# Rounding h0 on ScalarE instead of VectorE, and taking all of group 1's batch sums to VectorE, in a fused condition and feed-forward kernel

## What is computed

```python
# x: 32 batches x 64 rows x 512; cond: 32 x 256; W_fc: 2048 x 512; W_proj: 512 x 2048
q_emb = relu(cond @ W3 + b3)                       # one row of 512 per batch
x1    = (n * x + x.sum(axis=rows)) * q_emb         # n = 64 rows per batch
h0    = relu(x1 @ W2 + b2)
h     = square(relu(h0 @ ternary(W_fc).T))         # 2048 wide
hn    = h * rsqrt(mean(square(h)) + eps)
out   = x + hn @ ternary(W_proj).T
# ternary(w): groups of 64 weights; scale = mean |w|, q = clip(round(w / scale), -1, 1), result q * scale
```

## Time and profile before

| | |
|---|---|
| device time, median of 3 runs | 312.59 us (312.39 to 313.21) |
| device time of the profiled execution | 312.75 us |
| its span | 311.0 us |
| what lies around the span | 1.75 us (312.75 - 311.0) |
| TensorE (PE) busy | 305.5 us, 98% of the span |
| VectorE (DVE) busy | 188.7 us, 61% |
| ScalarE (ACT) busy | 191.1 us, 61% |
| GpSimd (POOL) busy | 102.0 us, 33% |

### The profile page before, as it was taken

How to read it: one execution, slowest core, us unless ns; L and a number is a source line. 1 busy time by engine, 2 the same in 40 slices (tenths; PEclk the granted TensorE clock), 3 DMA queues, 4 the chain that set the end, 5 groups by cost and what they waited for, 6 DMA issues and landing times.

```text
span 311.0 us, 3798 instructions
## 1 busy us (share of the span) xinstructions
PE 305.5 (98%) x1286; PEld 233.7 (75%) x1286; DVE 188.7 (61%) x318; ACT 191.1 (61%) x282; POOL 102.0 (33%) x94
## 2 busy tenths in 40 slices
PE   8999999999999999999999999999999999999995
PEld 7764545446888888888888888888888888888883
DVE  0589999995778877888348235952223484222245
ACT  1685366696999699977646554445555445555540
POOL 1012333345433223344342431253333314333330
PEclk9999999999999999999999999999999999999999
DMA  6999435443464041115004300340000033000003
GB/s 211 354 274 277 173 73 99 133 112 93 125 212 103 1 102 37 34 34 52 17 0 147 125 0 1 133 140 0 0 2 0 0 135 137 0 0 0 2 2 136
DMA packets 31332, 27.03 MB, mean 87 GB/s; under 512 B 18736, under 2 KB 20816, under 8 KB 31312
## 3 DMA queue, kind: packets, MB, share of 16 engines
q1 hardware_dynamic: 29936, 26.22, 29.8%
q10 hardware_dynamic: 1376, 0.56, 0.7%
HBM read 18.39 MB, written 4.19 MB: 73 GB/s over the span
## 4 chain that ended last, share of the span: by engine, by line
PE 98%; DVE 0%; issue 0%; POOL 0%; POOLq 0%; DVEq 0%
PE ps_out L360 37%; PE ps_acc L348 37%; PE ps_acc L332 18%; PE ps_out L310 2%; PE ps_out L319 1%; PE ps_acc L404 1%; PE ps_x L419 1%; PE ps_acc L411 0%; PE ps_x L394 0%; DVE x_sb L565 0%; DVE x_t L495 0%; PE ps_x L400 0%; PE ps_acc L407 0%; POOL ident_f L712 0%; POOL ident_f L710 0%
## 5 line engine op out<-in xcount | busy, mean ns | idle before, releaser
L243 POOL TENSOR_TENSOR wv_sb<-wv_sb 128x512 f32<-128x512 f32 x55 | 71.7, 1304 | 122.7 <-DVE y_lo L510 115.6
L348 PE MATMUL ps_acc<-h_hi,w_t 128*128 128x512 f32 x256 | 100.0, 391 | 0.0
L360 PE MATMUL ps_out<-w_t,y_hi 128*128 128x512 f32 x256 | 100.0, 391 | 0.0
L360 PE MATMUL ps_out<-w_t,y_lo 128*128 128x512 f32 x256 | 99.6, 389 | 0.0
L348 PE MATMUL ps_acc<-h_lo,w_t 128*128 128x512 f32 x256 | 99.6, 389 | 0.0
L508 DVE CAST y_hi<-x_t 128x512 fp32r<-128x512 f32 x64 | 33.2, 518 | 86.9 <-PE ps_out L360 70.2
L655 ACT ACTIVATE x_t<-ps_acc 128x512 f32<-128x512 f32 x64 | 37.8, 591 | 61.1 <-PE ps_acc L348 61.1
L332 PE MATMUL ps_acc<-x_t,wv_sb 128*128 128x512 f32 x128 | 56.3, 593 | 0.3 <-DVE x_t L495 0.3
L348 PEld LDWEIGHTS ps_acc<-h_lo,w_t 128*128 128x128 f32 x256 | 48.1, 188 | 10.2 <-issue 0.2
L348 PEld LDWEIGHTS ps_acc<-h_hi,w_t 128*128 128x128 f32 x256 | 48.1, 188 | 10.2 <-issue 0.2
L360 PEld LDWEIGHTS ps_out<-w_t,y_hi 128*128 128x128 f32 x256 | 48.1, 188 | 9.9
(11 more groups left out here) (61 smaller groups left out, 163.6 us busy)
## 6 DMA issues: line engine op xcount, KB each, us to landing
x_sb<-in_x_dram SPq DMA_DIRECT2D x5, 1024.0 KB, 5.3
raw<-in_L_ffn_W_fc_dram SPq DMA_DIRECT2D x8, 512.0 KB, 7.0
raw<-in_L_ffn_W_proj_dram SPq DMA_DIRECT2D x8, 512.0 KB, 4.2
out_dram<-x_sb SPq DMA_DIRECT2D x16, 256.0 KB, 2.1
x_odd<-in_x_dram SPq DMA_DIRECT2D x2, 1024.0 KB, 7.6
x_sb<-in_x_dram SPq DMA_DIRECT2D x4, 256.0 KB, 4.2
wv_sb<-in_L_cond_W_dram SPq DMA_DIRECT2D x4, 256.0 KB, 8.7
x_t<-in_L_cond_W_dram ACTq DMA_DIRECT2D x1, 512.0 KB, 4.6
```

The lines of the kernel that those rows point to most:

```text
L243: engine.tensor_tensor(acc, acc, y_sq[:, v % SQ_RING, :], ALU.add).then_inc(sq_added, 1)
L348: last = pe.matmul(ps_acc[:, (UNITS + v) % ACC_RING, :], w_t[:, j, k * P:(k + 1) * P], part[:, k, g * BANK:(g + 1) * BANK], start=(k == 0 ...
L360: last = pe.matmul(ps_out[:, t, :], part[:, v % RING, t * P:(t + 1) * P], w, start=(opens(v) and part is y_hi), stop=(closes(v) and part i ...
```

## The change

It has four parts. All of group 1 is transposed, with sums by VectorE (`sums_by_vector`). `round_h0` is gone: `relu_h0` on ScalarE reads the PSUM bank twice, once for `h0_hi` and once for `h0_f`, and VectorE keeps only a wait where its cast stood. Step 1 moves from unit 1 to unit 2, where it stands behind group 1's blocks. GpSimd's subtraction of unit u also waits until VectorE has done its work of unit u (`vector_through`).

```diff
-    STEP_AT_UNIT = {0: 0, 1: 1, 3: 2, 7: 3, 9: 4, 11: 5, 12: 6, 14: 7}
+    STEP_AT_UNIT = {0: 0, 2: 1, 3: 2, 7: 3, 9: 4, 11: 5, 12: 6, 14: 7}
...
     def sums_by_vector(g, k):
-        return g > 1 or g == 1 and k > 1
+        return g > 0
...
+    def blocks_scaled(u):
+
+        return KD + len([k for v in range(min(u + 1, UNITS - KD)) for k in SUMS_OF_UNIT[v // KD][v % KD]])
...
+        def vector_through(u):
+
+            steps = [v for v in STEP_AT_UNIT if v <= u]
+            last_scale = max([v for v in range(min(u + 1, UNITS - KD)) if SUMS_OF_UNIT[v // KD][v % KD]], default=-1)
+            if max(steps) >= last_scale:
+                return tern_ready, len(steps)
+            return x1_ready, blocks_scaled(u)
...
-            def round_h0(u):
-                g, m = u // KD, u % KD
-                dve.wait_ge(h0_relued, u + 1)
-                dve.tensor_copy(h0_hi[:, m, g * BANK:(g + 1) * BANK], h0_f[:, u % RING, :]).then_inc(h0_hi_done, 1)
-
...
                 if u > 0:
-                    round_h0(u - 1)
+
+                    dve.wait_ge(h0_relued, u)
...
-            round_h0(UNITS - 1)
...
             def relu_h0(u):
-                m = u % KD
+                g, m = u // KD, u % KD
                 act.wait_ge(h0_done, u + 1)
+                act.activation(h0_hi[:, m, g * BANK:(g + 1) * BANK], ps_acc[:, u % ACC_RING, :], ACT.Relu, bias=bv_t[:, m:m + 1]
+                               ).then_inc(h0_hi_done, 1)
                 wait(act, h0_split, u - RING + 1)
                 act.activation(h0_f[:, u % RING, :], ps_acc[:, u % ACC_RING, :], ACT.Relu, bias=bv_t[:, m:m + 1]
                                ).then_inc(h0_relued, 1)
...
                 pool.wait_ge(h0_hi_done, u + 1)
+                pool.wait_ge(h0_relued, u + 1)
+                pool.wait_ge(*vector_through(u))
```

## The result

| | before | after |
|---|---|---|
| median of the runs compared | 312.49 us (311.87 to 313.21, 4 runs) | 315.45 us (315.28 to 315.95, 4 runs) |
| profiled execution, its span | 312.75, 311.0 us | 315.28, 313.3 us |

The ratio is 1.0100, with a 95% interval from 1.0082 to 1.0118. The changed kernel is slower by 2.96 us; +2.23 was forecast, a time of 314.8 in a range of 313.4 to 316.3.

What follows compares the result with a forecast made beforehand. TensorE's own list of work, busy 98% of the span, was taken as the bound. Terms -0.91 + 1.36 + 0.69 + 0.70 + 0.39 = +2.23 us on 312.59 gave 314.8, range 313.4 to 316.3.

Steps and rivals of the forecast that it cites:

- The order on VectorE as the cause: On VectorE, pair 2's reduce and scales come behind group 1's four blocks, so ScalarE's w_scale and queued h0 hold TensorE.
- the first two stalls: TensorE waits for ScalarE's h0: 1.36 us at make_h0(5) and 0.69 at make_h0(6).
- handovers of 3.70 us: VectorE's reduce and scales, then ScalarE's w_scale and h0 writes: 1.49 + 0.96 + 0.58 + 0.67 us per turn.
- the small waits in the tiles (0.39): Two or three short TensorE stalls ahead of project(2), (4) and (6), together 2.23 - 1.84 = 0.39 us.
- the cover: At project of tile 6, TensorE could start at 100.14 and did at 100.66: 0.52 us taken off ScalarE's 2.75 delay.
- The unknown price: ScalarE's h0 write in fp32r, shown by no row: taken as 0.58 us, bounds 0.50 and 0.67, eleven on the path.
- The saving of 0.91: On TensorE, group 1's eight sum blocks become transposes, 0.87 us instead of 1.78, saving 0.91 in full.
- Rival C: GpSimd's subtractions and VectorE's blocks hinder each other: eight meetings of 0.2 us, +1.6 on top, 316.4; chance 0.05.
- Rival A: Only the stalls at make_h0(5) and make_h0(6) stay, VectorE catches up later: +1.14 us, 313.7; chance 0.07.
- B: No new stall, only TensorE's 0.91 us gain, 311.7, if pair 2's w_scale starts by 29.76; chance 0.10.
- What the forecast put at nothing: Group 3's blocks (1.2 us of cover), its x load issued at about 35.5, and GpSimd's new waits (3 us spare): no cost.
- the first line of the sum: First wait: from ScalarE's 19.02 and TensorE's 19.18, make_h0(5) starts at 33.47 against 32.11, a stall of 1.36 us.

Runs made afterwards that it cites:

- the changed kernel, second: The changed kernel repeated without any edit, timed against the kernel before: 315.57 us, ratio 1.0098; its profile has a span of 313.5 us.
- the last variant: Changed kernel with pair 2's reduce and scales ahead of group 1's blocks and VectorE's wait for h0 taken out: 311.97 us, ratio 0.9982 to the kernel before.

## Why the prediction was right, and its size a little short

*The order on VectorE as the cause: right.* Putting the scales ahead removed the first two stalls; moving the whole step moved the stall to the blocks; leaving the sums on TensorE removed everything.

*The working, place by place.* In the execution that started nearly where my sum did (the changed kernel, second), next to the first profile:

```
                              forecast    after    after, second
unit 0 starts                  12.08      10.97        12.21
w_scale of pair 2              31.12      30.92        31.19
ScalarE idle before it          7.8        7.88         7.88
make_h0(5)                     33.47      33.19        33.45
make_h0(6)                     38.47      38.12        38.39
hidden(1)                      77.13      76.94        77.22
project of tile 6             102.89     102.90       103.14
span                          313.2      313.3        313.5
```

(102.89 is the start of before and 2.23.) Every step of the sum is there, and after the handovers of 3.70 us each `hidden(1)` came 0.09 us from its forecast. The stalls as the waits show them are shorter than forecast (0.36 for 0.69 at `make_h0(6)`, 0.55 for 0.69 at `hidden(1)`), as TensorE's own work from a stall on took longer than I had it (4.57 us from `make_h0(5)` to the end of the transposes, where I had 4.31); the moments at which ScalarE lets it go on are those of the forecast.

The term of the sum that was too small is the last, the small waits in the tiles (0.39), and it was misread rather than measured short. I took from the chain that `project` of tile 6 started at 100.66 in the kernel before. But a piece of the chain begins where the record of the matmul before it ends, and these records overlap. The timeline of the same execution has the first matmul of that `project` 0.16 us earlier:

```profile
100.50 0.39 PE L360 MATMUL ps_out<-w_t,y_hi 128*128 128x512 f32 x1
```

So the cover was 100.50 - 100.14 = 0.36 us and not 0.52, the term 0.55, and the sum +2.39. The ways at nearly the same start (301.29 and 298.92) differ by 2.37, where spans are known to 0.1. In the chain of the changed kernel these waits show as pieces longer than the 1.81 us of one tile (3.62 of two):

```profile
76.94 3.96 PE ps_acc L360 x16
80.90 1.94 PE ps_out L372 x8
...
84.66 1.81 PE ps_out L372 x8
...
95.54 1.90 PE ps_out L372 x8
...
102.90 1.89 PE ps_out L372 x8
```

From `hidden(1)` to the `project` of tile 6 it was 25.96 and 25.92 us by the chain, where I had 25.76. A part of the first piece's 0.34 is the same overlap, which a piece that begins after a wait does not have. The small waits came at `project` of tiles 0, 4 and 6, where the forecast named 2, 4 and 6.

*The unknown price: right.* The new writes follow each other in 0.57 us and last 0.67, where I took 0.58 (and the estimate from the Trainium skill, ScalarE: Activation LUTs, What ACT_TABLE_LOAD costs, was 0.61). Over eleven writes the row was 0.1 us off and the page's figure 0.4 (0.04 x 11): the trace was the better source.

*The saving of 0.91: right*, and it is what remains as a gain where nothing stalls: the way of the last variant is 309.9 - 11.95 = 297.95, against 298.92.

*Rival C: right that this contention exists, wrong that the change brings it.* A meeting costs 1.0 us and not 0.2, and the pairing prevents all of them on the path. Rival A did not happen: `hidden(1)` waits. B needed `w_scale` by 29.76; in the changed kernel it started at 30.92, and only variants that shorten or reorder VectorE's work ahead of it have it in time (28.64 with the sums back, 29.50 without VectorE's wait, 23.49 and 23.07 with the scales ahead).

*What the forecast put at nothing* did cost nothing. The second load of x into `x_odd`, for group 3, was issued at 35.45 (about 35.5 in the forecast), and the waits of the changed kernel have no row of TensorE matmuls for a load or for GpSimd in the unit phase.

*What was short: 2.96 against 2.23.* The mechanism holds; three sizes were off. The first is the term of the small waits, 0.16 short as shown above. The second is the first line of the sum, which took the start of both engines from one execution. The changed kernel is bound by ScalarE, whose list begins with loads of weights. The chain of waits of the first profile begins so, and TensorE is not in it before 76.94:

```profile
4.33 8.72 DMA raw<-in_L_ffn_W_fc_dram
13.04 0.02 issue
13.07 1.06 ACT w_abs L623
...
18.76 0.67 ACT h_hi L656
...
21.25 0.70 DVE batch_sum L500
```

An early TensorE is worth nothing to it any more. The kernel before is bound by TensorE from its first unit, so an early start should make it shorter by as much; its three profiles all began near 12.1, and none shows an early one. (The variant with the sums back, bound the same way, began at 12.57, with 311.4 - 12.57 = 298.83 to its end.) The median span over ten executions of the changed kernel is 313.5, that of the kernel before 310.6 to 310.8 in the three groups: 2.7 to 2.9 in the span. Of that, 2.37 is the sum of my steps at the same start. The median span of the kernel before is 0.2 to 0.4 below that of its profile; early starts that the changed kernel swallows would explain this, which is argued and not shown.

The third lies outside the span: the time is longer than the span by 1.79 to 1.82 us (medians) in the kernel before and in the variant with the rounding on VectorE, and by 2.01 to 2.06 in the changed kernel and its six other variants. These 0.2 us go with the edits that the rounding variant takes back (ScalarE's second write and GpSimd's waits); which of them, and why outside the span, stays open. 2.37 + 0.2 to 0.4 + 0.2 is 2.8 to 3.0.

## What to carry to other kernels

Where two engines that work in order hand something over in a loop, ask of each wait what else is queued behind it. ScalarE had 7.9 us to spare and still held TensorE up, since the short operation that released it (1.5 us of scales) stood behind 8.2 us of work that could wait; putting that short one first was worth 2.2 us (315.45 to 313.27), moving the whole step with it nothing in the median (315.48). A change that moves the bound from one engine's list to another's also changes which start-up jitter counts, so set the start from several executions. And a wait that looks needless in the data may keep two engines off each other. Here one of the two was worth 3.1 us (GpSimd's, 315.45 to 318.58 without it) and the other cost 2.7 (VectorE's, 315.45 to 312.73): try each taken out, with the profile beside it, before you remove it.

## What the runs showed of the hardware

- VectorE multiplies of two SBUF inputs and casts from SBUF lasted up to about a microsecond longer when a GpSimd `tensor_tensor` (1.27 us) lay beside them: an fp32 multiply 1.71 for 0.69, a bf16 one 1.64 for 0.69, two casts 2.07 for 0.75. Operations that read PSUM beside the same GpSimd work kept their 0.69. The reduce of |w|, with one input from SBUF, was not held either: 1.22 us at 33.17 in the changed kernel, beside the subtraction at 33.27, and 1.21 without one.
- ScalarE writes h0 in fp32r as fast as in fp32 (0.67 each, 0.57 from start to start).
- The same program (the changed kernel) starts unit 0 at 10.97, 11.51 or 12.21 us from one execution to the next.
